# A quarter of every twentieth gather of a graph layer moved from GpSimd's indirect DMAs to one-row DMAs of SyncE

## The reference

```python
nodes = node_state[edges].reshape(num_edges, -1)      # [x[src], x[dst]], 128 wide
gates = ssp(edge_state @ We1 + be1) @ We2 + be2
gates = gates * (1.0 - sigmoid(5.0 * (edges_distance - 3.5)))
h = ssp(nodes @ Wn1 + bn1) @ Wn2 + bn2
message_sum = zeros_like(node_state).at[edges[:, 1]].add(h * gates)
new_state = node_state + (ssp(message_sum @ Ws1 + bs1) @ Ws2 + bs2)
out = layernorm(x + new_state)
```

## Time and profile before

| what | value |
|---|---|
| median of 3 runs | 1991.86 us (1990.89 to 1994.37) |
| the profiled execution: its span | 1988.8 us |
| POOL busy | 1484.7 us (75%), 1572 instructions |
| PE busy | 1737.7 us (87%) |
| ACT, DVE busy | 1532.1 us (77%), 1285.6 us (65%) |
| POOL's 1564 gathers | 1483.7 us busy, 949 ns each, 477.6 us idle before them |
| moved by all DMAs | 157.78 MB, 79 GB/s |

### The profile page before, as it was taken

The page is one execution under the profiler, slowest core; times in us unless marked ns, Lnnn a source line. Parts: engine busy times, 40 slices in busy tenths (PEclk is TensorE's granted clock), DMA queues, the critical chain, the costliest instruction groups (busy, mean ns, idle before and its releaser), DMA issues.

```text
span 1988.8 us, 53540 instructions
## 1 busy us (share of the span) xinstructions
PE 1737.7 (87%) x16249; PEld 1328.7 (67%) x16249; DVE 1285.6 (65%) x3512; ACT 1532.1 (77%) x3368; POOL 1484.7 (75%) x1572
## 2 busy tenths in 40 slices
PE   4699999898888988878889988998988898988987
PEld 3577777676666666666666766766666676766666
DVE  4578888666665655555656666666666666666666
ACT  3589999777777777777777788788777787787877
POOL 7777777777777777777777777777777777777773
PEclk7799999999999899999989999899999899999999
DMA  5433333333333333333333333333333233333331
GB/s 122 122 85 98 97 97 97 85 85 76 91 74 73 71 73 70 75 68 71 74 71 74 74 80 74 74 75 78 74 75 75 69 84 75 75 78 75 75 76 38
DMA packets 256432, 157.78 MB, mean 79 GB/s; under 512 B 45401, under 2 KB 227046, under 8 KB 256366
## 3 DMA queue, kind: packets, MB, share of 16 engines
q1 hardware_dynamic: 202652, 104.94, 18.2%
q0 software_dynamic: 50048, 51.35, 15.5%
q10 hardware_dynamic: 3666, 0.68, 0.2%
HBM read 146.94 MB, written 9.87 MB: 79 GB/s over the span
## 4 chain that ended last, share of the span: by engine, by line
POOL 57%; issue 22%; PE 11%; DVE 3%; ACT 2%; SPq 2%; DMA 2%; DVEq 1%; ACTq 1%; POOLq 0%
POOL ga L459 57%; PE ps L623 3%; PE ps L636 3%; PE ps L640 1%; DVE hid L1113 1%; SPq L340 1%; PE ps L585 1%; DMA ga<-in_x_dram,srcT 1%; PE ps L575 1%; DVE hid L1117 1%; PE ps L653 1%; PE ps L662 1%; PE ps L577 0%; DVEq L1139 0%; ACT lg L861 0%
## 5 line engine op out<-in xcount | busy, mean ns | idle before, releaser
L459 POOL DMA_INDIRECT ga<-in_x_dram,srcT x1564 | 1483.7, 949 | 477.6 <-issue 472.4
L852 ACT ACTIVATE lg<-ps,bn1c 128x512 f32<-128x512 f32 x391 | 268.4, 687 | 306.6 <-PE ps L585 267.6
L636 PE MATMUL ps<-wn,hid 128*128 128x64 f32 x3128 | 447.9, 288 | 18.9 <-DVE hid L1117 17.1
L1113 DVE SCALAR_TENSOR_TENSOR hid<-ps,neg_b,lg 128x512 f32<-128x512 f32 x391 | 292.8, 749 | 221.9 <-ACT lg L867 205.2
L636 PEld LDWEIGHTS ps<-wn,hid 128*128 128x128 f32 x3128 | 393.1, 197 | 51.5 <-DVE hid L1117 26.6
L575 PE MATMUL ps<-ident,ea 128*128 128x128 f32 x782 | 173.8, 305 | 198.2 <-DMA ga<-in_x_dram,srcT 135.2
L844 ACT COPY xe<-ps 128x512 f32<-128x512 f32 x391 | 229.9, 588 | 113.3 <-PE ps L577 99.8
L623 PE MATMUL ps<-xe,wn 64*128 64x256 f32 x1564 | 289.8, 449 | 0.0
L1151 DVE TENSOR_TENSOR acc<-acc,ps 64x64 f32 x782 | 168.4, 215 | 163.7 <-issue 157.9
L640 PE MATMUL ps<-we,hid 128*128 128x128 f32 x1564 | 273.1, 299 | 0.0
L575 PEld LDWEIGHTS ps<-ident,ea 128*128 128x128 f32 x782 | 80.0, 143 | 282.1 <-issue 268.8
(11 more groups left out here) (124 smaller groups left out, 1847.9 us busy)
## 6 DMA issues: line engine op xcount, KB each, us to landing
ea<-in_edge_attr_dram SPq DMA_DIRECT2D x195, 256.0 KB
ga<-in_x_dram,srcT POOLq DMA_INDIRECT x1564
bw<-b_tab SPq DMA_DIRECT2D x782, 32.0 KB
relb<-rel_tab SPq DMA_DIRECT2D x196, 64.0 KB
b_tab<-share SPq DMA_DIRECT2D x25, 250.0 KB
out_dram<-xs SPq DMA_DIRECT2D x25, 125.0 KB
xs<-in_x_dram SPq DMA_DIRECT2D x3, 750.0 KB
rows_i<-in_dst_dram SPq DMA_DIRECT2D x1, 768.0 KB
```

Source lines behind the costliest of these rows:

```text
L459: pool.indirect_dma_start(to[:, t % 2, t // 2, :], None, x, bass.IndirectOffsetOnAxis(ap=idx[:, t:t + 1], axis=0)).then_inc(done, 16)
L636: pe.matmul(hg[:, t * D:(t + 1) * D], hid[:, u % 2, t * P:(t + 1) * P], wn2[:, :], start=False, stop=False, skip_group_check=True)
L852: act.activation(lg[:, u % 2, 0:QUAD].rearrange("p (k e) -> p k e", k=2), z[:, :, 0:PAIR], ACT.Abs, bias=bn1c[:, 0:1]).then_inc(n_abs, 1)
L1113: dve.scalar_tensor_tensor(out=hid[:, u % 2, 0:QUAD].rearrange("p (k e) -> p k e", k=2), in0=ps[:, 2 * (u % 2):2 * (u % 2) + 2, 0:PAIR], s ...
```

## The change

Every twentieth quad from 40 to 360 (17 quads, `ROW_QUADS`), POOL issues three gathers instead of four. The fourth group of 128 rows is fetched by SP: 128 DMAs of one row (256 bytes) each into a new buffer `stage` (two halves, used in turn), and then one DMA from `stage` to the quad's place in `ga`. The 128 are dealt out over ten pairs (`ROWS_TURN`: 12 rows a pair, 16 in two of the ten), in `load_rows`, which stands behind the pair's `ea` DMA. The first set starts at quad 16, the last ends at quad 354; set i is handed over by `hand_rows` at the pair of quad 36 + 20 i. POOL waits for the hand-over (`handed`) before the third gather of such a quad.

The row addresses: SP loads the 17 x 128 indices of `src` with one DMA of single elements into the first partition of `rows_i` (before its first pair, after waiting for all 12 counts of `row_e`), DVE multiplies them by 256, and SP loads 12 or 16 of them into registers at a time. The `bw` places are now stored as byte addresses (`wb_all`, with a table, a store and a load of its own on ACT's queue), so that their fused multiply goes. SP's loops over pairs are written out.

```diff
+ROWS0 = 40
+ROWS_EVERY = 20
+ROWS_N = 17
+ROWS_BEFORE = 24
+ROWS_TURN = (12, 12, 12, 12, 16, 12, 12, 12, 12, 16)
...
+        stage = sb("stage", [P, 2, D])
+        row_at = rows_i[0:1, :, :, :].rearrange("p a g e -> p (a g e)")[:, 0:ROWS_N * P]
...
-                    sp.dma_start(bw[n % 2 * W:(n % 2 + 1) * W, v + n // 2, :],
-                                 b_tab[bass.ds(first, W), :]).then_inc(s_bw[v], 16)
+                    sp.dma_start(bw[n % 2 * W:(n % 2 + 1) * W, v + n // 2, :].bitcast(U8),
+                                 b_bytes[bass.ds(first, W * F * 4)].rearrange("(r b) -> r b", b=F * 4)).then_inc(s_bw[v], 16)
+            def load_rows(q):
+                i, turn = divmod(q - (ROWS0 - ROWS_BEFORE), ROWS_EVERY)
+                turn //= 2
+                if not (q >= ROWS0 - ROWS_BEFORE and i < ROWS_N):
+                    return
+                if i == 0 and turn == 0:
+                    sp.wait_ge(row_ready, 1)
+                if i >= 2 and turn == 0:
+                    sp.wait_ge(xe_t, ROW_QUADS[i - 2] + 1)
+                first, n = ROWS_FIRST[turn], ROWS_TURN[turn]
+                _, places = nc.values_load_multi_w_load_instructions(
+                    row_at[:, i * P + first:i * P + first + n], engines=(mybir.EngineType.SP,), min_val=0,
+                    max_val=(N - 1) * D * 4, skip_runtime_bounds_check_because=IN_X)
+                for r, place in enumerate(places):
+                    sp.dma_start(stage[first + r:first + r + 1, i % 2, :].bitcast(U8),
+                                 x_bytes[bass.ds(place, D * 4)].rearrange("(r b) -> r b", r=1)).then_inc(s_stage[i % 2], 16)
+            def hand_rows(q):
+                i = (q - (ROWS0 - 4)) // ROWS_EVERY
+                if (q - (ROWS0 - 4)) % ROWS_EVERY or not 0 <= i < ROWS_N:
+                    return
+                quad = ROW_QUADS[i]
+                sp.wait_ge(s_stage[i % 2], P * 16 * (i // 2 + 1))
+                sp.wait_ge(xe_t, quad - (ARING - 1))
+                sp.dma_start(ga[:, quad % ARING, 1, 1, :], stage[:, i % 2, :]).then_inc(handed, 16)
...
                 if reached(q, RING):
                     load_ea(q, u)
+                load_rows(q)
+                hand_rows(q)
...
             with sp.Else():
+                sp.wait_ge(row_e, XCOLS)
+                sp.dma_start(row_at.rearrange("p (i e) -> p i e", e=P),
+                             src[ROWS0 * QUAD:(ROWS0 + ROWS_N * ROWS_EVERY) * QUAD].rearrange(
+                                 "(a i e) -> a i e", a=1, e=ROWS_EVERY * QUAD)[:, :, PAIR + 1:QUAD:2]).then_inc(ld_row, 16)
                 for q in range(BRING):
                     fast_step(q, q)
...
+                if q in ROW_QUADS:
+                    gather(to, idx, 0, done)
+                    gather(to, idx, 1, done)
+                    pool.wait_ge(handed, 16 * (ROW_QUADS.index(q) + 1))
+                    gather(to, idx, 2, done, 32)
+                else:
+                    gather_rows(to, idx, done)
...
+                dve.wait_ge(ld_row, 16)
+                dve.tensor_scalar(row_at, row_at, float(D * 4), None, ALU.mult).then_inc(row_ready, 1)
```

More of the change, by code:

```diff
@@ L25 @@
 BRING = 8
+ROWS0 = 40
[3 more added lines that the diff above has]
+ROWS_TURN = (12, 12, 12, 12, 16, 12, 12, 12, 12, 16)
+ROWS_FIRST = tuple(sum(ROWS_TURN[:n]) for n in range(len(ROWS_TURN)))
 IN_RANGE = "windows' places are the least of N - W and of destinations, which are nodes"
+IN_X = "sources are nodes"
 def reached(i, n):
@@ L85, in gnn_layer @@
     assert RG > 1 and RL > 1
+    ROW_QUADS = [ROWS0 + ROWS_EVERY * i for i in range(ROWS_N)]
+    assert sum(ROWS_TURN) == P and all(n % 4 == 0 for n in ROWS_TURN) and 2 * len(ROWS_TURN) == ROWS_EVERY
+    assert ROWS0 % 2 == 0 and ROWS0 + ROWS_EVERY * ROWS_N <= FULL and ROW_QUADS[-1] < NQ - 8
     STEPS = 8
@@ L260, in gnn_layer @@
         g_oh, g_mm, g_add = ([sem(f"{n}{k}") for k in range(2)] for n in ("g_oh", "g_mm", "g_add"))
+        ld_row, row_ready, wb_ready, wb_stored = (sem(n) for n in ("ld_row", "row_ready", "wb_ready", "wb_stored"))
+        handed = sem("handed")
+        s_stage = [sem(f"s_stage{k}") for k in range(2)]
         filled, hg_set = sem("filled"), sem("hg_set")
@@ L367, in _ @@
                 share_stored(0, g)
-            sp.wait_ge(w_loaded, 16)
+            sp.wait_ge(w_loaded, 32)
             sp.wait_ge(rel_stored, 32)
@@ L378, in fast_step @@
                 _, firsts = nc.values_load_multi_w_load_instructions(
-                    w_all[0:1, bass.ds(q * 2, 2 * n)], engines=(mybir.EngineType.SP,), min_val=0, max_val=N - W,
+                    wb_all[0:1, bass.ds(q * 2, 2 * n)], engines=(mybir.EngineType.SP,), min_val=0, max_val=(N - W) * F * 4,
                     skip_runtime_bounds_check_because=IN_RANGE)
@@ L414, in _ @@
                     load_x(n)
-                for q in range(BRING, 2 * BRING):
-                    fast_step(q, q % BRING)
[L419 to L441, removed]
+                ahead = NODE0 + STEPS
+                for q in range(BRING, NQ):
+                    stored, made, node = (q - 12) // 4, (q - 7) // 4, (q - (ahead + STEPS - 1)) // STEPS
+                    if q % 4 == 0 and 1 <= stored < NG:
+                        share_stored(stored // 2, stored % 2)
+                    fast_step(q, q % BRING)
+                    if q % 4 == 3 and SHARES <= made < NG:
+                        store_share(made, made % 2)
+                    if q % STEPS == (ahead - 1) % STEPS and 0 <= node < EARLY:
+                        store(node)
             for g in range(EARLY, NG):
@@ L454, in _, with gather @@
             pool.iota(iota_pi[:, :], pattern=[[1, 1]], base=0, channel_multiplier=1).then_inc(iotas, 1)
+            def gather(to, idx, t, done, inc=16):
+                pool.indirect_dma_start(to[:, t % 2, t // 2, :], None, x,
+                                        bass.IndirectOffsetOnAxis(ap=idx[:, t:t + 1], axis=0)).then_inc(done, inc)
             def gather_rows(to, idx, done):
                 for t in range(4):
-                    pool.indirect_dma_start(to[:, t % 2, t // 2, :], None, x,
-                                            bass.IndirectOffsetOnAxis(ap=idx[:, t:t + 1], axis=0)).then_inc(done, 16)
+                    gather(to, idx, t, done)
             def fast_step(q):
@@ L471, in fast_step @@
                     pool.wait_ge(xe_t, q - (ARING - 1))
-                gather_rows(ga[:, q % ARING], srcT[:, 4 * q:4 * q + 4], s_ga[q % ARING])
+                to, idx, done = ga[:, q % ARING], srcT[:, 4 * q:4 * q + 4], s_ga[q % ARING]
+                if q in ROW_QUADS:
[5 more added lines that the diff above has]
+                    gather_rows(to, idx, done)
             def general_step(q, u):
```

12 lines of the change are left out of this document (11 added, 1 removed).

## The result

The changed kernel takes 2042.92 us (median of 4 runs, 2042.11 to 2045.25) where the kernel before takes 1993.11: a ratio of 1.0249, 95% interval 1.0237 to 1.0262. It is 50 us slower. I forecast slower, but 2273 us: the loss came out at 50 us and not at 280. The direction was right, the size wrong.

The account below looks back on a forecast made before the run. POOL's gathers bound the kernel before; SP would take over at 11.36 us a pair: 153.8 + 1931 + 8 + 151.6 + 25.7 = 2270 us of span, plus 3 gives 2273 us; 8-in-10 range 2010 to 2480.

Parts of the forecast that it names:

- P: SP's work for one pair of quads: 5.34 us before, forecast 11.36 after (ends 9.0 and 15.3), above POOL's 10.0.
- register load: SP's load of 12 or 16 row addresses a pair: 1.89 us, from DVE's eight-word load plus a gap.
- delay of the start: SP's single-element index load on one engine holds the first pair, so PE's first `front` starts 33 us late.
- the sum's formula: Span: start of quad 16's pair, 170 pairs of P, last hand-over, POOL's remaining 121 gathers, tail: 2270 us.
- 12.8 one-row DMAs with `MOVE`s: SP's row fetches in a pair, 0.37 us each with `MOVE` and gaps: 4.74 us (ends 3.65 and 7.97).
- all else in a pair: SP's earlier work in a pair, 5.34 us, less 0.66 us for eight instructions that go.
- hand-over: SP's DMA into `ga`, about 0.5 us once in ten pairs: 0.05 us a pair.
- rival 3: Full queues make SP's one-row DMAs dearer, P 13 to 15.3: 2550 us at 13, 2940 at the end; 12%.
- main case: SP never waits and sets the pace from quad 16 to 354, P 10.2 to 12.5: 2073 to 2465 us; 61%.
- rival 2: SP keeps up but starts late, P 9.0 to 9.7: 2015 us, up to 2073 at P 10.2; 19%.
- Rival 1: SP keeps up at P 9.0, no late start, one 14.7 us stall at quad 40: 1982 us span; 8%.

Follow-up runs that it names:

- e19: Changed kernel with row sets every 24th quad from 40 on, 14 sets, 10.7 rows a pair: 2004.87 us, ratio 1.0043 to the kernel before.
- e15: Changed kernel with row sets every 24th quad from 72 on, 13 sets, 10.7 rows a pair: 1975.38 us, ratio 0.9917 to the kernel before.
- e12: Changed kernel with two fifths of PE's matmuls left out: 2040.66 us, where the kernel before with the same matmuls left out takes 1990.56.

## Why the prediction was wrong in size

The mechanism was the predicted one: SP without slack, every engine at its pace, POOL handed its rows late, POOL's own pace again behind quad 360. The step that failed is the size of SP's work P, in it the register load above all, and next the delay of the start. The profiled span follows the sum's formula, with measured values: 131.7 + 170 x 10.125 + 9.9 + 151.3 + 26.2 = 2040.3 us. (The 9.9 us are not all SP's: at quad 360 itself POOL no longer waits, its third gather follows the one before after 0.31 us.) The steps:

| term | forecast, us | measured, us | worth over 170 pairs |
|---|---|---|---|
| 12.8 one-row DMAs with `MOVE`s | 4.74 | 4.28 | -78 |
| register load of 12 or 16 words, with what follows it | 1.89 | 1.02 | -148 |
| all else in a pair | 4.68 | 4.77 | +15 |
| hand-over | 0.05 | 0.06 | +2 |
| P | 11.36 | 10.12 | -210 |
| delay D of the pair of quad 16 | 33 | 10.9 | -22 |

The measured parts are the distances from each SP instruction to the next over the 170 pairs, added up by line. -210 and -22, with +2 at the end behind quad 356, make the 230 us between the forecast span of 2270 and the real 2040.3. P was 12% too large. But what costs time is its excess over what the kernel before takes for the same 170 pairs, 9.77 us each with the fast start, and that was 1.59 us by my P and is 0.35 measured.

**The register load failed most.** I took DVE's 1.844 us for eight words and left the number at that for twelve on SP. Both loads as the changed kernel has them:

```profile
L372 SPq TENSOR_LOAD <-rows_i x170: 921/940/1197, 137.9 to 1845.8; - x170
...
L429 SPq TENSOR_LOAD <-wb_all x196: 459/561/1643, 37.9 to 1997.4; - x196
...
L376 SPq DMA_DIRECT2D stage<-in_x_dram x2176: 224/228/318, 139.0 to 1852.0; - x198
```

Most of these loads have twelve words, the median of 0.940 us, and sixteen take up to 1.197: 0.06 us a word. The row that would have told it was SP's own: four words took 0.332 us at the least. I had two rows, one of the right engine and the wrong size, one of the wrong engine and a nearer size, and took the latter. The engine was the thing to match. The Trainium skill's 200 ns a register ("Runtime: NRT & Kernel Launch", Instruction fetch mechanics) would give 2.4 us by its figure, an estimate; the 0.940 us of this row does not agree with it.

**The one-row DMAs.** 0.228 us each, against 0.239 and 0.252, and 0.335 from one to the next with the `MOVE`, not 0.37: most of the difference is the DMA itself, the rest are gaps smaller than the 45 ns that I took from `bw`. The full-queue price of rival 3 never appeared; the largest of 2176 is 0.318 us.

**The start.** I had one engine at 17 ns an element, 37 us. `relb` was held for 13.1 us. In the DMA view of 38.5 to 52 us this queue moves 2117 packets in 8.8% of 16 engines' time:

```profile
q1 hardware_dynamic: 2117, 0.01, 8.8%
```

0.088 x 16 x 13.5 / 2117 = 9.0 ns a packet, half of the 17 that I had from ACT's queue. That row was a poor source: its 3666 packets are 0.68 MB, 185 bytes each in the mean and not 4, and its share of 0.2% is rounded. And the 19 us of work lie in 13.5, so more than one packet was under way at a time. The Trainium skill's rule that gave an engine count of 1 ("DMA: Bandwidth & Descriptors", Why a DMA increments its semaphore by 16 and not by 1) would by an estimate, 2176 packets of 9.0 ns one behind the other, make this 19.6 us; from the DMA's start at 37.05 to the end of the held `relb` at 51.84 there are 14.8, and no run here shows how many engines took part. PE's first `front` starts at 56.0 us, not near 80.

**The rivals.** P came out at 10.12, just under the 10.2 at which I let the main case begin, and D between its ends. The time lies in the band that I gave to rival 2 (2015 to 2073 us, 19%), and within my 8 in 10 range, but SP did not keep up as rival 2 has it: it set the pace. Rival 1 was the right picture of what a smaller P does: its stall at quad 40 is `e19`, and its gain without the stall is `e15`. But its limit, P below 9.4, holds only for a first set at quad 40, where the stall has to stay below the 21.3 us saved: `e15`, with its first set at quad 72, gains with 9.56.

**What I had not said** is where the loss is made. I set P against POOL's 10.0 us a pair and thought of a steady drain; the trace shows nearly all of it made before quad 106, while the kernel before ran at 8.5 us a pair.

## What to carry to other kernels

When work moves to an engine that only issues, add up its time for one turn of the loop from its own records, gap by gap, and price a new instruction by a row of the same engine before one of the same size. Its slack must be compared with the fastest stretch of the loop, not with the mean: here 10.1 us a pair against 10.0 cost 50 us, since the ramp ran at 8.5. The same move with a sixth fewer rows a pair and a later first set gained 16 us. And a test that takes work off an engine has to be checked by that engine's busy time: two fifths of PE's matmuls were gone, and its busy time was not.

## What the runs showed of the hardware

- A stall of the engine that bounds the kernel is kept to the end, here within about 2 us: 28.1 us once in `e19`, +8.4 us in the time after 17.5 saved.
- With 9993 matmuls in place of 16249, PE was busy 1751 us in place of 1798 (`e12` and the changed kernel): its mean granted clock was 0.57 in place of 0.92.
- A register load of SP costs 0.06 us for each further word: 0.940 us for twelve, up to 1.197 for sixteen. A one-row DMA holds SP for 0.228 us.
- 2176 single elements held the next DMA of the same queue for 13.1 us; as one run, not at all.
- Two chips took 2505 us (medians) for a kernel that takes 1992 to 1996 us on the others, with the gathers at 945 to 949 ns in its variants, as in the kernel before (949), and PE at a granted clock of 0.82 to 0.85, and made some variants 23 and 33% slower. What a profile says of the bound on such a chip is not to be carried to another.
